# Two fused transformer layers with a product-key stage: the expert choice kept in PSUM, the normalised rows handed to the feature maps in halves across the border of two rounds, four score banks in the last layer-1 pass

## Chip, cores and metric

One core of one Trainium2 chip runs the kernel. The metric is the device time of one execution in microseconds (us), the median of several. TensorE is called PE here, its sequencer PEq and its weight loads PEld, VectorE DVE, ScalarE ACT, GpSimd POOL and SyncE SP, as in the profile.

## What is computed

The input x is 4 batches of 512 rows of 128 numbers. Four blocks follow one another, each with a residual and a layer norm behind it (all float32 in and out):

```python
x = _layernorm(x + _L0_attn_ref(x, ...))   # gated attention in groups of 32 rows, plus a linear part over the batch
x = _layernorm(x + _L0_ffn_ref(x, Wg, We)) # 8 experts, the 2 best per row, weighted
x = _layernorm(x + _L1_attn_ref(x, ...))   # 16 heads of 8, causal linear attention on softmax features
x = _layernorm(x + _L1_ffn_ref(x, ...))    # product keys: top 8 of 32 x 32, rows of down and up
```

In the expert block, `logits = x @ Wg`, the gate is a softmax over 8 experts, the two largest are kept and divided by their sum, and the row's output is the sum of the two chosen experts' products. In the causal attention each head maps q and k by `softmax(p)` and `softmax(-p)` to 16 features, and row t reads the running sum of k (x) v up to t. The last block begins with a batch norm, whose mean and variance run over all 2048 rows.

## The kernel before

The file has two functions with one block of hand-ordered instruction streams each, one stream per engine, which meet by semaphores only. `layers` (lines 184 to 1470) does the first three blocks for all batches, `peer` (from 1474) the last. `layers` takes 320 of the 587 us and is what the change touches.

A batch is T = 4 tiles of 128 rows. Functions `a_*` belong to the gated attention and the experts (layer 0), `b_*` to the causal attention (layer 1). After a prologue that takes batch 0 through layer 0, four rounds follow, `for s in range(1, B + 1)`: round s takes batch a = s through layer 0 and batch b = s - 1 through layer 1, interleaved by hand in each of the four streams. Round 4 has no batch a: it is the lone round. A stream is in order: an instruction that waits holds all that are behind it on its engine.

PSUM has 8 banks. What matters of a round:

- Border. DVE closes batch a with `a_experts(a, p)` (L822, two tiles per p: `z2 = z2 + bank * wexp`, 8 experts), then the norm of z2 (`a_z2`, `a_x2`, L726 to L736, with a `pow` on POOL between, L573), and batch b with `b_y`, `b_z3`, `b_z3_spread`, `b_x3`. PE transposes x2 (`b_x2t`, L1205), ACT copies it, PE multiplies by the combined weights (`b_qkv`, L1217, banks 4 to 7), ACT copies the maps to `pm` (`b_maps`, L414).
- Maps. DVE takes minimum and maximum over each head's 8 numbers (L845, L846), subtracts (L847); POOL subtracts for the negative half (`b_negative`, L600); ACT takes the exponential (`b_exp`, L434); DVE sums, inverts and multiplies to `feat` (`b_features`, L855 to L857). All this for two halves of two tiles.
- In the meantime ACT and PE prepare batch a: `a_qk`, `a_heads` (L359, L369), `a_val`, `a_gate` (L383, L377), `a_sim`, `a_link` (L389), `a_kv` (L1144), `a_outt` (L1153).
- Transposes and low parts. PE transposes features (`b_transposes`, L1231, L1236), ACT copies high halves (L454), DVE computes the low halves `q_lo` (`b_low_queries`, L873).
- Scores. For each tile u and each row group g, PE computes a 128 x 512 score block (`b_scores`, L1267) into bank 4 or 5, DVE masks it (`b_masked`, L883), ACT casts its high half (L463), POOL subtracts for the low half (`b_low_scores`, L622), PE multiplies both with the values (`b_numerators`, L1282 to L1295), DVE sums (`b_summed`, L904). `b_products` and `b_states` (L891, L896) carry the running state from tile to tile.
- Choice. Behind `a_x1`, PE multiplies by Wg (`a_logits`, L1183, bank 1), `a_shift` takes the 8 largest and their places (L786, L792) and marks hits against an iota tile (L797, L799), `a_choice` turns them into weights (L805 to L810). All their small tiles (128 x 32) are in SBUF but the logits. PE computes the experts of tiles 0 and 1 (`a_experts`, L1196) before the second half of `b_scores(b, 2)`.

DVE operations depend on one another through `step`, a semaphore of the engine's own.

## Time and profile before

| | us |
|---|---|
| median of 3 runs | 590.48 (590.31 to 592.97) |
| the profiled execution: its time | 589.03 |
| its span | 587.3 |
| DVE busy | 490.6 (84%) |
| PE busy | 411.7 (70%), mean granted clock 0.764 of 2.4 GHz |
| ACT busy | 317.9 (54%) |
| POOL busy | 189.2 (32%) |

Of the time 1.7 us lie outside the span. A granted clock of 0.50 is 1.2 GHz, 1.00 is 2.4 GHz. In the rows further below, a stretch is given by its start and end from the span's start; a line of a timeline has its start, its duration, engine, line, operation, output<-inputs with their shapes, how many, and in brackets the idle time ahead of it with what ended it. Buffer numbers are left out there, so z and z2, x1 and x2, masked0 (called masked) read alike, and `feat` also holds the masked scores of odd tiles. In the trace the rounds begin at about 66, 134, 200 and 264 us, and `peer` at 320 us.

### The profile page before, as it was taken

The numbers are of one execution on the slowest core, as the hardware profiler recorded it, in microseconds if no ns is written. First come the engines' busy times: TensorE is split into PE (matmuls) and PEld (weight loads), VectorE is DVE, ScalarE is ACT, GpSimd is POOL, SyncE is SP. The second block draws the span as 40 slices with busy tenths as digits, with TensorE's granted clock in tenths as the row PEclk, the third lists the DMA queues.
The fourth block names the chain that finished last, engine by engine and source line by source line (L and its number), as shares of the span: only waits on it lengthen the run. The fifth ranks groups of instructions, "written<-read, shape, count | busy, mean of one in ns | idle before, by whom it ended". The sixth has DMA issues, their size and how long they took to land. (4 is left out here: it accounts for less than half of the span.)

```text
span 587.3 us, 12452 instructions
## 1 busy us (share of the span) xinstructions
PE 411.7 (70%) x4560; PEld 291.7 (50%) x4560; DVE 490.6 (84%) x2056; ACT 317.9 (54%) x639; POOL 189.2 (32%) x211
## 2 busy tenths in 40 slices
PE   1769869986998779854574637576847676767585
PEld 0455548644865467532473214353725354545475
DVE  3586699898999899987854799699979999999991
ACT  0602565346533664314641537767586868688591
POOL 4550224823194416813482230303030303030000
PEclk9998987698859976887755955685959595957577
DMA  7220000000000000000000000000000000000000
GB/s 200 73 61 0 1 2 2 2 1 0 2 0 3 0 2 1 2 1 0 1 2 0 2 1 1 2 2 11 2 10 2 12 2 11 2 11 1 12 2 19
DMA packets 12459, 6.72 MB, mean 11 GB/s; under 512 B 3182, under 2 KB 11758, under 8 KB 12398
## 3 DMA queue, kind: packets, MB, share of 16 engines
q1 hardware_dynamic: 10566, 4.34, 2.8%
q10 hardware_dynamic: 1832, 1.58, 1.0%
q8 instruction: 36, 0.59, 0.4%
q14 instruction: 25, 0.20, 0.1%
HBM read 4.87 MB, written 1.05 MB: 10 GB/s over the span
## 5 line engine op out<-in xcount | busy, mean ns | idle before, releaser
L1665 ACT ACTIVATE hot_last<-iota_f,lo_last 128x128 f16<-128x128 f32 x256 | 75.8, 388 | 0.3 <-DVE lo_last L1789 0.3
L1806 DVE TENSOR_TENSOR hot_lo<-lo_t,iota_lo 128x4096 f16<-128x4096 f16 x24 | 53.6, 2286 | 0.3
L1927 PE MATMUL psum<-hot_w,hot_lo 128*128 128x16 f16 x1536 | 43.6, 172 | 14.0 <-DVE hot_lo L1806 14.0
L1927 PEld LDWEIGHTS psum<-hot_w,hot_lo 128*128 128x128 f16 x1536 | 41.9, 101 | 20.6 <-DVE hot_lo L1806 19.6
L1893 PE MATMUL psum<-x3t,down_t 128*128 128x512 f32 x64 | 42.6, 768 | 13.3 <-ACT hid L1631 11.6
L1579 POOL TENSOR_TENSOR eq<-eq,side_f 128x1024 f16<-128x1024 f16 x14 | 28.9, 2083 | 55.5 <-DVE eq L1767 55.5
L1267 PE MATMUL psum<-q_hi,k_t 32*128 32x128 f16 x256 | 38.0, 259 | 9.8 <-DVE masked L883 6.4
L1587 POOL TENSOR_TENSOR rstd<-rstd,minus_half 128x2 f32<-128x2 f32 x8 | 5.6, 701 | 114.0 <-DVE rstd L1836 114.0
L622 POOL TENSOR_TENSOR s_lo<-masked,s_hi 128x512 f16<-128x512 f32 x32 | 36.5, 1170 | 16.5 <-ACT s_hi L463 12.8
L1736 DVE FIND_INDEX8 side_i<-side,keysims 128x8 uint32<-128x32 f32 x256 | 41.5, 185 | 0.0
L1196 PE MATMUL psum<-we,x1t 128*128 128x512 f32 x64 | 40.1, 777 | 0.4 <-DVE z L822 0.4
L1927 PE MATMUL psum<-hot_w,hot_last 128*128 128x16 f16 x512 | 14.9, 174 | 36.0 <-issue 28.6
L1267 PE MATMUL psum<-q_lo,k_t 32*128 32x128 f16 x256 | 38.2, 261 | 0.0
L1940 PE MATMUL psum<-upw,mix 128*128 128x128 f32 x256 | 36.9, 306 | 1.1 <-DVE mix L1821 1.1
L573 POOL TENSOR_TENSOR a_rstd<-a_rstd,minus_half 128x4 f32<-128x4 f32 x8 | 8.1, 1013 | 90.3 <-DVE a_rstd L731 90.3
L1927 PEld LDWEIGHTS psum<-hot_w,hot_last 128*128 128x128 f16 x512 | 14.4, 104 | 45.1 <-issue 45.1
L622 POOL TENSOR_TENSOR s_lo<-feat,s_hi 128x512 f16<-128x512 f32 x32 | 36.2, 1158 | 1.4 <-ACT s_hi L463 1.4
L1940 PEld LDWEIGHTS psum<-upw,mix 128*128 128x128 f32 x256 | 35.5, 222 | 1.5 <-DVE mix L1821 1.5
L1267 PEld LDWEIGHTS psum<-q_hi,k_t 32*128 32x128 f16 x256 | 25.1, 113 | 17.4 <-DVE masked L883 9.1
L463 ACT CAST s_hi<-masked 128x512 f16<-128x512 f32 x32 | 19.4, 618 | 25.9 <-DVE masked L883 24.9
L1882 PE MATMUL psum<-keysim,xn 128*128 128x512 f32 x32 | 29.1, 1008 | 4.9 <-ACT keysims L1624 4.9
L1893 PEld LDWEIGHTS psum<-x3t,down_t 128*128 128x128 f32 x64 | 13.4, 236 | 35.8 <-ACT hid L1631 23.7
(265 smaller groups left out, 1186.2 us busy)
## 6 DMA issues: line engine op xcount, KB each, us to landing
xall<-in_L_attn_x SPq DMA_DIRECT2D x4, 256.0 KB, 6.9
out<-o SPq DMA_DIRECT2D x8, 128.0 KB, 1.9
we<-in_L_ffn_We SPq DMA_DIRECT2D x1, 512.0 KB, 4.0
downn<-in_L_ffn_down SPq DMA_DIRECT2D x1, 512.0 KB, 5.4
upw<-in_L_ffn_up SPq DMA_DIRECT2D x1, 512.0 KB, 6.5
wh<-in_L_attn_W_h SPq DMA_DIRECT2D x1, 256.0 KB, 4.5
keysn<-in_L_ffn_keys_p ACTq DMA_DIRECT2D x1, 256.0 KB, 10.9
wqkv<-in_L_attn_w_qkv ACTq DMA_DIRECT2D x1, 192.0 KB
```

What stands on the lines that cost most here:

```text
L463: nc.scalar.copy(s_hi[:, u % 2, g, :], masked[u % 2][:, g, :]).then_inc(shi_ok.h, 1)
L622: nc.gpsimd.tensor_tensor(s_lo[:, u % 2, g, :], masked[u % 2][:, g, :], s_hi[:, u % 2, g, :], ALU.subtract).then_inc(slo_ok.h, 1)
L1196: ins = nc.tensor.matmul(bank[Y_BANK[u] + k][:], x1t[:, P * u:P * u + P], v.we[:, 4 * k:4 * k + 4, :].rearrange("p e m -> p (e m)"), start ...
L1267: ins = nc.tensor.matmul(bank[4 + g % 2][:, P * c:P * c + P], k_t[r, u, c, :], q[r, u, c, :], start=(q is q_hi), stop=(q is q_lo))
L1579: nc.gpsimd.tensor_tensor(hit, hit, bc(side_f[:, u % 4].rearrange("p i r h -> p (i r) h").unsqueeze(3), [P, 2 * K, NH, K]), ALU.mult)\
L1665: ins = nc.scalar.activation(hot_last[:, lane], iota_f[:], ACT.Abs, bias=lo_last[:, lane:lane + 1], scale=-1.0)
L1736: ins = nc.vector.max_index(side_i[:, u % 4, s, :], side[:, u % 4, s, :], keysims[:, u % 4, s, :])
L1806: nc.vector.tensor_tensor(hot_lo[:, pairs], bc(lo_t[:, lanes].rearrange("p (j s) -> p j s", s=2).unsqueeze(2), [P, LB // 2, P, 2]), bc(v.i ...
L1882: nc.tensor.matmul(bank[6][:], xn[:, P * (u % T):P * (u % T) + P], v.keysim[:].rearrange("p s k -> p (s k)"), start=True, stop=True)\
L1893: nc.tensor.matmul(bank[H_BANK(b, c)][:], v.down_t[:, c, :], v.x3t[:, N * b:N * b + N], start=True, stop=True).then_inc(h_mm.h, 1)
L1927: ins = nc.tensor.matmul(bank[2 + q][:, c:c + 2 * EH], low, hot_w[:, i, lane // 2, :, :, lane % 2].rearrange("p t e -> p (t e)"), start=(i ...
L1940: nc.tensor.matmul(bank[0][:, P * t:P * t + P], mix[:, EH * t + e, :], v.upw[:, e, :], start=(e == 0), stop=False)
```

## The change

1. **The choice in PSUM.** `logits`, `hits`, `chosen`, `gate_sum` and an iota are slices of bank 6; the iota is put there in each round by a small product in front of the logits. One addition becomes a reduction over the two hits. Logits wait for `b_states` to be through with bank 6, and the experts' second tile no longer waits for the places to be found. `b_states` masks in three pieces, two of them in place in PSUM, and adds from there.
2. **x2 in halves.** `a_z2`, `a_x2`, `b_x2t` and `b_qkv` take a half p (two tiles); x2 has two buffers; the maps' products go to banks 0, 1 (half 0) and 4, 5 (half 1). Half 0 is normalised, transposed and multiplied before the round's end. `b_z3`, its norm and `b_x3`, `b_moments` of batch b - 1 move into the next round, between the halves of the maps. z3 goes to bank 6, the moments read SBUF. ACT takes `a_qk`, `a_heads`, `a_val` and `a_gate` of batch a between the two exponentials, POOL takes `b_negative` before `a_heads`.
3. **The lone round.** Scores use banks 4, 5, 0, 1, and DVE computes the low halves of groups 2 and 3 (`b_low_scores` on DVE), POOL those of 0 and 1 alone.

```diff
+    QKV_BANK = (0, 1, 4, 5)
+    S_BANK = ((4, 5, 4, 5),) * (B - 1) + ((4, 5, 0, 1),)
...
+        logits, iota_t, chosen = (bank[6][:, T * E * k:T * E * k + T * E].rearrange("p (t e) -> p t e", t=T) for k in (0, 1, 4))
+        hits = bank[6][:, 2 * T * E:4 * T * E].rearrange("p (j t e) -> p j t e", j=2, t=T)
+        gate_sum = bank[6][:, 5 * T * E:5 * T * E + T]
...
-                        ins = nc.vector.tensor_tensor(hits[:, j], iota, bc(topi[:, :, j:j + 1], [P, T, E]), ALU.is_equal)
+                        ins = nc.vector.tensor_tensor(hits[:, j], iota_t, bc(topi[:, :, j:j + 1], [P, T, E]), ALU.is_equal)
                     step(ins)
-                    step(nc.vector.tensor_tensor(chosen[:], hits[:, 0], hits[:, 1], ALU.add))
+                    step(nc.vector.tensor_reduce(chosen, hits.rearrange("p j t e -> p t e j"), X, ALU.add))
...
+                def b_low_scores(u):
+
+
+                    for g in (2, 3):
+                        wait(dve, shi_ok, B - 1, 4 * u + g + 1)
+                        nc.vector.tensor_tensor(s_lo[:, u % 2, g, :], masked[u % 2][:, g, :], s_hi[:, u % 2, g, :],
+                                                ALU.subtract).then_inc(slo_last_ok.h, 1)
...
                 def b_states(b):
 
                     wait(dve, st_mm, b)
...
+                    nc.vector.tensor_tensor(state[:, 0], raw[0], own_heads, ALU.mult)
                     for u in range(1, T - 1):
-                        ins = nc.vector.tensor_tensor(state[:, u], state[:, u], state[:, u - 1], ALU.add)
+                        ins = nc.vector.tensor_tensor(raw[u], raw[u], own_heads, ALU.mult)
+                    step(ins)
+                    for u in range(1, T - 1):
+                        ins = nc.vector.tensor_tensor(state[:, u], raw[u], state[:, u - 1], ALU.add)
...
                 def a_logits(b):
 
                     wait(pe, x1t_ok, b)
+                    if b:
+                        wait(pe, st_ok, b - 1)
...
+                    nc.tensor.matmul(iota_t, ones16[:], iota_rows[:], start=True, stop=True)
...
                 def a_experts(b, u):
 
-                    if u == 1:
-                        pe.wait_ge(found_ok.h, b + 1)
-                    elif u == 2 and b:
+                    if u == 2 and b:
...
+                def b_x2t(b, p):
+
+                    if b and p == 0:
+                        wait(pe, sums_ok, b - 1, 3)
+                    for u in (2 * p, 2 * p + 1):
                         wait(pe, x2_ok, b, u + 1)
...
+                def b_transposes(b, u):
+
+                    if u == 0 or u == 2:
+                        wait(pe, twice_ok, b, u // 2 + 1)
+                    if u == 0:
+                        wait(pe, v_ok, b)
```

DVE around the border of rounds 1 and 2, from the sum z3 of batch b to the first maps, before:

```order
L920 TENSOR_TENSOR z<-x,psum 128x512
L726 BN_STATS a_stats<-z 128x6 x4
L729 BN_AGGR a_mv<-a_stats 128x2 x4
L731 TENSOR_SCALAR a_rstd<-a_mv 128x4
L726 BN_STATS b_stats<-z 128x6 x4
L729 BN_AGGR b_mv<-b_stats 128x2 x4
L731 TENSOR_SCALAR b_rstd<-b_mv 128x4
L736 TENSOR_SCALAR x<-z,a_mv,a_rstd 128x128 x4
L736 TENSOR_SCALAR x<-z,b_mv,b_rstd 128x128 x4
L936 BN_STATS bn_raw<-psum 128x6
L845 TENSOR_REDUCE pmin<-pm 128x64
L846 TENSOR_REDUCE pmax<-pm 128x64
```

and with the change, from the y of batch b on:

```order
L946 TENSOR_TENSOR y<-pe_in,den 128x512
L842 SCALAR_TENSOR_TENSOR z<-psum,wexp,x 128x128 x2
L842 SCALAR_TENSOR_TENSOR z<-psum,wexp,z 128x128 x14
L744 BN_STATS a_stats<-z 128x6 x2
L747 BN_AGGR a_mv<-a_stats 128x2 x2
L749 TENSOR_SCALAR a_rstd<-a_mv 128x2
L865 TENSOR_REDUCE pmin<-pm 128x64
L866 TENSOR_REDUCE pmax<-pm 128x64
L867 TENSOR_TENSOR pe_in<-pm,pmax 128x64x8
L754 TENSOR_SCALAR x<-z,a_mv,a_rstd 128x128 x2
L953 TENSOR_TENSOR z<-x,psum 128x512
L875 TENSOR_REDUCE psum_<-pe_in 128x128
```

In front of these rows the change has the statistics of z2's tiles 0 and 1 and their x2; z3's norm, x3 and the moments follow behind the first features.

ACT behind yt (the copy of the transposed y) at the same border, before:

```order
L478 COPY yt<-psum 128x512
L359 ACT_TABLE_LOAD
L359 ACTIVATE qk_t<-psum,bqk_col 128x512
L369 ACTIVATE heads_t<-qk_t,bet,gam 128x512 x2
L383 ACTIVATE val<-psum 128x512
L377 ACTIVATE gate_t<-psum,bh_gate 128x512
L383 ACTIVATE val<-psum 128x512
L409 COPY x2t<-psum 128x512
L483 COPY x3t<-psum 128x512
L414 COPY pm<-psum 128x512 x2
L377 ACTIVATE gate_t<-psum,bh_gate 128x512
L434 ACT_TABLE_LOAD
```

and with the change:

```order
L487 COPY yt<-psum 128x512
L443 ACTIVATE pe_in<-pe_in 128x1024
L416 COPY x2t<-psum 128x256
L365 ACT_TABLE_LOAD
L365 ACTIVATE qk_t<-psum,bqk_col 128x512
L375 ACTIVATE heads_t<-qk_t,bet,gam 128x512 x2
L422 COPY pm<-psum 128x512
L449 ACTIVATE k<-feat 128x32x16
L451 COPY feat<-feat 128x2x16x16
L389 ACTIVATE val<-psum 128x512
L383 ACTIVATE gate_t<-psum,bh_gate 128x512
L389 ACTIVATE val<-psum 128x512
```

The copy of pm, which the first exponential needs, now stands ahead of these rows. Behind them come one more gate, an ACT_TABLE_LOAD and only then the second exponential, the values and the link; before, the second exponential followed the first with four copies between.

DVE in the lone round, from the masks of tile 0 to those of tile 2, with the change:

```order
L905 TENSOR_TENSOR masked<-psum,causal 128x512 x4
L915 TENSOR_TENSOR s_lo<-masked,s_hi 128x512 x2
L905 TENSOR_TENSOR feat<-psum,causal 128x512 x4
L924 TENSOR_TENSOR state<-psum,same_quad 128x144
L926 TENSOR_TENSOR psum<-psum,same_quad 128x144 x2
L929 TENSOR_TENSOR state<-psum,state 128x144 x2
L915 TENSOR_TENSOR s_lo<-feat,s_hi 128x512 x2
L905 TENSOR_TENSOR masked<-psum,causal 128x512 x4
```

Before, the rows `s_lo` are not in this stream: all 16 were on POOL.

## Rows read from the trace of the kernel before

**Rows 1.** Busy time by stretch: us, PE, PEld, DVE, ACT, POOL busy, PEclk, DMA, GB/s.

```profile
226.90:240.40 13.50, 13.42 (x102) 8.95 (x100) 13.07 (x32) 5.41 (x10) 13.22 (x12) 0.57 0.01 1
240.40:251.20 10.80, 9.15 (x162) 6.76 (x160) 9.96 (x26) 3.57 (x6) 6.78 (x6) 1.00 0.01 2
121.93:127.50 5.57, 3.44 (x17) 1.88 (x15) 5.47 (x19) 3.13 (x4) 0.00 (x0) 1.00 0.00 1
121.93:150.79 28.86, 21.38 (x89) 13.63 (x88) 25.96 (x63) 16.70 (x26) 8.54 (x8) 0.88 0.00 1
251.20:284.19 32.99, 14.88 (x82) 9.51 (x80) 27.03 (x68) 13.32 (x23) 6.59 (x6) 0.79 0.00 0
284.19:308.12 23.93, 17.45 (x300) 15.37 (x300) 15.34 (x24) 10.71 (x18) 19.89 (x18) 0.54 0.01 2
322.00:587.00 265.00, 174.83 (x2567) 123.94 (x2565) 233.75 (x1387) 181.27 (x412) 50.68 (x63) 0.70 0.02 6
```

**Rows 2.** VectorE groups 66 to 322 us: count | busy, mean ns | idle before.

```profile
L847 DVE TENSOR_TENSOR pe_in<-pm,pmax 128x512 f32<-128x512 f32 x8 | 8.6, 1076 | 0.3
L896 DVE TENSOR_TENSOR state<-state 128x144 f32<-128x144 f32 x8 | 8.1, 1016 | 0.3
L797 DVE TENSOR_TENSOR hits<-iota_e,topi 128x32 f32<-128x32 f32 x6 | 5.8, 999 | 0.1
...
L845 DVE TENSOR_REDUCE pmin<-pm 128x64 f32<-128x512 f32 x8 | 5.4, 679 | 7.3 <-ACT pm L414 7.3
L799 DVE TENSOR_TENSOR chosen<-hits 128x32 f32<-128x32 f32 x3 | 3.2, 1080 | 0.1
L936 DVE BATCH_NORM_STATS2 bn_raw<-psum 128x6 f32<-128x512 f32 x4 | 2.8, 698 | 4.4 <-ACT x3t L483 4.4
L810 DVE TENSOR_TENSOR wexp<-chosen,lsum 128x32 f32<-128x32 f32 x3 | 2.7, 895 | 0.1
```

**Rows 3.** VectorE timeline, prologue: start, us, instruction.

```profile
49.10 0.29 DVE L797 TENSOR_TENSOR hits<-iota_e,topi 128x32 f32<-128x32 f32 x2
```

**Rows 4.** TensorE timeline, middle of round 3.

```profile
233.75 6.01 PE L1196 MATMUL psum<-we,x1t 128*128 128x512 f32 x8
```

**Rows 5.** VectorE timeline, middle of round 3.

```profile
240.40 1.29 DVE L883 TENSOR_TENSOR masked<-psum,causal 128x512 f32<-128x512 f32 x2
250.09 1.11 DVE L904 TENSOR_REDUCE pe_in<-psum 128x144 f32<-128x432 f32 x2
```

**Rows 6.** GpSimd timeline, middle of round 3.

```profile
244.44 4.50 POOL L622 TENSOR_TENSOR s_lo<-feat,s_hi 128x512 f16<-128x512 f32 x4 [0.35 <-ACT s_hi L463]
```

**Rows 7.** ScalarE timeline, border of rounds 1 and 2.

```profile
126.92 1.52 ACT L369 ACTIVATE heads_t<-qk_t,bet,gam 128x512 f32<-128x512 f32 x2
...
129.99 0.69 ACT L377 ACTIVATE gate_t<-psum,bh_gate 128x512 f32<-128x512 f32 x1 [0.32 <-PE psum L1105]
...
134.15 0.58 ACT L483 COPY x3t<-psum 128x512 f32<-128x512 f32 x1 [1.12 <-PE psum L1316]
...
139.03 1.28 ACT L434 ACT_TABLE_LOAD   x1
140.32 1.06 ACT L434 ACTIVATE pe_in<-pe_in 128x1024 f32<-128x1024 f32 x1
```

**Rows 8.** TensorE timeline, the kv product in rounds 1 and 2.

```profile
76.07 1.99 PE L1144 MATMUL psum<-val,link 128*128 128x256 f32 x8 [2.62 <-ACT link L389]
...
142.18 3.12 PE L1144 MATMUL psum<-val,link 128*128 128x256 f32 x8 [2.62 <-ACT link L389]
146.88 2.08 PE L1153 MATMUL psum<-attn_t,val 128*128 128x128 f32 x8 [1.58 <-DVE attn_t L755]
```

**Rows 9.** VectorE timeline, first low queries in rounds 1 and 2.

```profile
84.69 0.68 DVE L873 SCALAR_TENSOR_TENSOR q_lo<-psum,q_hi 128x512 f16<-128x512 f32 x1
...
150.79 0.68 DVE L873 SCALAR_TENSOR_TENSOR q_lo<-psum,q_hi 128x512 f16<-128x512 f32 x1
```

**Rows 10.** VectorE timeline, last sum of the lone round.

```profile
307.51 0.61 DVE L904 TENSOR_REDUCE pe_in<-psum 128x144 f32<-128x432 f32 x1 [2.95 <-PE psum L1295]
```

More of the change, by code:

```diff
@@ L517, in _ @@
                 a_exp(0)
-                a_qk(1)
-                a_heads(1)
+                b_x2t(0, 0)
                 key_products()
+                b_maps(0, 0)
+                b_values(0, 0)
                 act.wait_ge(pads.h, 2)
@@ L523, in _ @@
                     a, b = s, s - 1
+                    b_exp(b, 0)
+                    b_x2t(b, 1)
+                    if a < B:
+                        a_qk(a)
+                        a_heads(a)
+                    b_maps(b, 1)
+                    b_features(b, 0)
                     if a < B:
@@ L569, in _, with root @@
             def _(pool):
-                def root(var_ok, root_ok, rstd, b, k):
+                def root(var_ok, root_ok, rstd, b, k, tiles=slice(0, T)):
                     wait(pool, var_ok, b, k)
-                    nc.gpsimd.tensor_tensor(rstd[:], rstd[:], bc(v.minus_half[:].unsqueeze(1), [P, T, 1]), ALU.pow)\
+                    nc.gpsimd.tensor_tensor(rstd[:, tiles], rstd[:, tiles],
+                                            bc(v.minus_half[:].unsqueeze(1), [P, tiles.stop - tiles.start, 1]), ALU.pow)\
                         .then_inc(root_ok.h, 1)
@@ L620, in b_low_scores @@
                     for g in groups:
+                        if b == B - 1 and g >= 2:
+                            continue
                         wait(pool, shi_ok, b, 4 * u + g + 1)
@@ L711, in _ @@
                     if a < B:
-                        root(a_var, a_root, a_rstd, a, 2)
-                    root(b_var, b_root, b_rstd, b, 1)
+                        for p in range(2):
+                            root(a_var, a_root, a_rstd, a, 2 + p, slice(2 * p, 2 * p + 2))
+                root(b_var, b_root, b_rstd, B - 1, 1)
             @block.vector
@@ L1133, in a_link @@
                     wait(pe, lin_ok, b, 1)
+                    wait(pe, val_ok, b)
                     for u in range(T):
```

305 lines of the change are left out of this document (169 added, 136 removed).

## Prediction

> **What bounds the kernel now.** I read the page first: DVE is busy 84% of the span, PE 70% at a mean granted clock of 0.764. Then the busy times by stretch, which say what each stretch hangs on. `peer` lasts 265 us (322 to 587, [rows 1]) and is not touched, so all of the difference must arise in the first 320 us. There I cut each round in two. The middle runs from the last x1 to the last of the four sums; in round 3 it is the first two stretches of [rows 1], 13.50 and 10.80 us. The border runs from there to the first `q_lo` of the next round: the fourth stretch, 28.86 us. What follows up to x1 keeps its order, and I cost it at nothing. The lone round is the fifth stretch (border and maps, 32.99 us) and the sixth (scores, 23.93 us).
>
> In the first part of the middle DVE looks full, 13.07 of 13.50 us, but so does PE, 13.42 of 13.50, at a granted clock of 0.57, mostly 1.2 GHz. The PE timeline shows why that matters: the experts take 6.01 us from 233.75 [rows 4], and the scores of tile 2, groups 2 and 3, stand behind them. They come at 240.3, and DVE masks them at 240.40 [rows 5]. The two engines arrive together; a faster DVE would only wait.
>
> In the border DVE is busy 25.96 of 28.86 us. Its waits are those for ACT's `pm`, 7.3 us, and for x3t, 4.4 us, over four borders [rows 2].
>
> **The change, part by part.** *The choice.* A hit costs 999 ns, the addition behind it 1080, the last product 895 [rows 2], while in the prologue two hits take 0.29 us together [rows 3], 0.15 each. Here POOL runs its subtractions all the while (13.22 of 13.50 us busy); there it does not. These rows read two operands from SBUF, while those with a PSUM operand, as the 128x512 mask, keep 0.65 us each beside POOL [rows 5]. The state additions are alike, 1016 ns for 144 columns [rows 2]. With one operand in PSUM I take 0.15 to 0.25 us each: 6 x 0.85 + 3 x 0.9 + 3 x 0.7 = 9.9 us less for the three kinds, and 8 x 0.77 = 6.2 for the states, less 1.6 for the instructions added. That is 14 us of DVE work at least. No row has an output in PSUM; at worst such an instruction stays at 1 us and nothing is saved.
>
> What of it lies on the path is another matter. The experts start behind a chain of PE work at 1.2 GHz: x1 transposes, scores, logits, scores, numerators. All of it stays, in its order; the iota product adds 0.1 us, and the wait of the logits for the states another 0.1. So the masks of 240.40 come when they came, and DVE waits some 4 us ahead of them. From there DVE gets 0.9 us of new work (statistics of two z2 tiles) in front of the last two sums, which it reached at 250.09 [rows 5], 1.2 us after POOL's last subtraction (248.94, [rows 6]): there is no slack for it. Three middles: 3 x 0.9 less small waits = **+2.2 us**. Bounds: +2.9 if nothing is hidden; -6 if PE were no bound, since POOL's own 20.0 us (13.22 + 6.78, [rows 1]) and 2.1 behind it would leave 22.3 of 24.3 us.
>
> *The border.* The halves take both waits out of it: x2's first half is ready before y, and `pm` comes during y and the experts. But ACT's queue has a new order. Call S the end of the last sum and M the end of the first maps. x2 of half 0 with its `pow` 0.8, y and experts 5.57 [rows 1], half a norm 0.9, maps 2.4 (0.68 twice, and 1.08 of L847 [rows 2]): M = S + 9.7. From M ACT must do an exponential (1.06), the copy of half an x2t (0.5), an ACT_TABLE_LOAD (1.28), qk (0.69), two heads (1.52), pm (0.55), two copies of features (1.1), val, gate, val, gate (2.5), a load (1.28), the second exponential (1.0) [rows 7]: 11.4 us. Values and link, 0.8, come next, and only then PE can do kv, the first `a_outt` and the transposes. In round 2 kv took 3.12 and outt 2.08 us, in round 1 kv took 1.99 at 2.4 GHz [rows 8]. With 1.3 for the transposes and 0.6 for `q_hi` that gives M + 19.0 at the lower clock and M + 16.7 at the higher one. I take the lower: PE is idle for some 3.5 us behind `a_sim`, waiting for `a_heads` on POOL, and in round 2 the row with 2.62 us of idle ahead of it is the slow one. S + 28.7 against 28.86 before: **0 us** for the borders of rounds 1 to 2 and 2 to 3; bounds -2.5 each (higher clock) and +2.2 (two copies or a product more in front of the exponential). DVE itself would be ready at M + 15.3, so it waits for `q_lo` in place of `pm`.
>
> *Prologue and round 1.* DVE now waits for the `pow` of half 0 (1.2 us) before the second experts; maps end near 68.0. With 19.0 less 0.5 (no x3t) the first `q_lo` comes at 86.5, at the higher clock at 84.5; before it was 84.69 [rows 9]. I take **+1.5 us**, bounds -0.2 and +3.7.
>
> *Lone round, border.* No layer-0 work stands in ACT's queue, so DVE sets the pace. Before: 32.99 us with 27.03 busy [rows 1], waits 6.0. After: 27.0 less 0.9 (statistics done earlier) plus 0.4 (norms cut in two), and waits of 0.3 (pow), 0.5 (exponential), 0.9 (last two `q_hi`) and 0.4 of issue: 28.6. **-4.4 us**, bounds -5.5 and -3.
>
> *Lone round, scores.* POOL is busy 19.89 of 23.93 us, and the last sum waits 2.95 us for the numerators behind it [rows 1, 10]. POOL loses 8 x 1.13 us (a quarter of 4.50, [rows 6]); DVE gets 8 x 0.6, loses 1.4 in the states, and has 15.34 + 4.8 - 1.4 = 18.7 of work, 1.2 of waits for `s_hi` and 1.7 of numerators at the end: 21.6. But the eight read two SBUF operands beside POOL, and [rows 2] show what that costs: 0.8 us more each at worst for four of them, 24.4. I take the middle, 23.0: **-1.0 us**, bounds -2.3 and +0.5.
>
> The Trainium skill has a rule that speaks against this part (SBUF - State Buffer, "SBUF: two separate sides"): DVE with two SBUF inputs and POOL lock each other out of a shared port for a whole instruction. By that rule the low halves don't run side by side, and the term is +0.5 in place of -1.0. The 999 ns hits fit it; no row has 128x512 subtractions on both engines.
>
> *Sum:* 2.2 + 0 + 1.5 - 4.4 - 1.0 = **-1.7 us**. The profiled execution took 589.03 us and would take 587.3; it lies 1.45 under the median of the runs shown, 590.48, so against that median I forecast **588.8 us**.
>
> **Rivals.** *A, the freed DVE time does arrive.* If PE gets the higher clock through the middle, or through the border, POOL and DVE are the bounds: middles -6 in place of +2.2, borders -5 and -0.2 in place of 0 and +1.5. All of it is -16.6 us, 573.9; half of it, which I hold likelier, about 581. For: PE would have fewer idle stretches at the borders. Against: in three rounds alike the clock was low through the scores and most of the experts (0.57 in [rows 1]). 0.32.
>
> *B, ACT's queue is the new bound, slower than before.* It decides when the second exponential ends later than M + 13: val and gate wait for PE products, which stand behind `b_qkv`, which waits for the x2t copy. Two more microseconds there, in three borders (+2.2, +2.2, and +3.7 in round 1), and the sum is -1.7 + 6.6 = +4.9: 595.4. For: four activations and a table load now stand ahead of it, where four copies stood. 0.17.
>
> *C, the port.* As the term above: +0.5 in the lone round's scores in place of -1.0, 590.3. DVE and POOL alternate. The rule of the skill named there says so. 0.07.
>
> *D, the choice gets no shorter in PSUM.* It lies behind PE as before, so the time stays the forecast's; it is inside the main case.
>
> **How the numbers follow.** Main case 0.44, its own range 585.5 to 592. A difference of 0.5% (2.95 us) is about what a measurement of this kernel tells from none; the bounds are 587.5 and 593.4. Of the main case 0.06 lies under 587.5 and 0.02, its unlikely upper end, over 593.4. Faster 0.06 + 0.32 = 0.38; slower 0.02 + 0.17 = 0.19; same 0.44 - 0.08 + 0.07 = 0.43. The range reaches from half of A to B's value: 580 to 595.5; what is left out is the full A and B's tail.
>
> **What would show it.** Right: hits, additions and states on DVE at 0.15 to 0.3 us; a new wait of 3 to 5 us on DVE ahead of the second masks of tile 2, ended by PE's L1267 counterpart; a wait of 2 us or more ahead of the first `q_lo`, ended by ACT; almost none ahead of pmin; the lone round's border near 28.6 us and its scores near 23. Wrong: x1-to-x1 of rounds 2 and 3 more than 2 us away from 65.8 and 64.7 us; a granted clock of 1.00 through the experts; DVE low halves of 1.5 us or more; `peer` other than 265 us.

## The result, and the profile after

| | before | changed |
|---|---|---|
| median | 591.73 us (4 runs, 590.31 to 593.08) | 582.87 us (4 runs, 580.88 to 586.18) |
| ratio | | 0.9867, 95% interval 0.983 to 0.9904 |
| a second series | 590.33 us (23 runs) | 585.09 us (6 runs, 581.27 to 587.34), ratio 0.9892, 0.9843 to 0.9941 |
| profiled execution: time, span | 589.03, 587.3 us | 583.85, 582.1 us |

The change makes the kernel 1.1 to 1.3% faster: some 5 to 9 us, where 1.7 were forecast. The range, 580 to 595.5, holds it; the central case (own range 585.5 to 592) does not. Ratios are worked out from fast runs alone; one of the fillers kernel's executions further down, at a mean granted clock of 0.55, took 669 us and is not among them.

First the head of the page after. DVE lost 8.5 us of work (490.6 before), although it took over 8.5 us of low halves (4.5 and 4.0, below); PE lost nothing.

```profile
span 582.1 us, 12503 instructions
## 1 busy us (share of the span) xinstructions
PE 411.8 (71%) x4564; PEld 293.6 (50%) x4564; DVE 482.1 (83%) x2076; ACT 314.8 (54%) x643; POOL 182.2 (31%) x208
```

Then the busy times by stretch, cut at the same events as [rows 1]: middle of round 1, border behind it, middle and border of round 2, middle of round 3, the lone round's border and its scores, and the stage `peer`. The columns are those of [rows 1].

```profile
98.30:122.60 24.30, 23.09 (x261) 15.75 (x259) 18.42 (x66) 8.87 (x16) 20.58 (x19) 0.73 0.01 1
122.60:148.90 26.30, 20.20 (x86) 13.72 (x87) 25.27 (x61) 15.95 (x27) 8.21 (x8) 0.87 0.00 0
160.40:184.40 24.00, 23.18 (x260) 16.30 (x260) 18.41 (x66) 8.69 (x16) 20.58 (x19) 0.67 0.01 2
184.40:210.50 26.10, 19.78 (x89) 12.84 (x88) 25.27 (x60) 15.93 (x27) 8.19 (x8) 0.93 0.00 0
222.00:246.10 24.10, 23.28 (x261) 16.33 (x260) 18.52 (x66) 8.69 (x16) 20.59 (x19) 0.67 0.01 2
246.10:274.60 28.50, 16.29 (x89) 10.78 (x89) 26.41 (x63) 13.15 (x24) 6.93 (x6) 0.71 0.00 0
274.60:299.10 24.50, 16.14 (x300) 14.83 (x295) 21.64 (x34) 10.70 (x18) 11.37 (x10) 0.50 0.01 2
311.30:582.10 270.80, 175.86 (x2568) 124.75 (x2568) 234.99 (x1393) 181.95 (x415) 51.85 (x66) 0.69 0.02 6
```

Against before: border 28.9 to 26.3 and 26.1, lone border 33.0 to 28.5, lone scores 23.9 to 24.5, middles 25.4, 24.2, 24.2 to 24.3, 24.0, 24.0 (the windows above are cut to 0.1 us). The last sum of the layers ends at 299.1 us where it ended at 308.1: 9.0 us won. From there to the end it takes 283.0 us where it took 279.2: 3.8 us given back, nearly all in `peer`, of which no instruction was touched.

The groups of DVE answer to [rows 2]: the hits cost 195 ns (999 before), the additions of states 307 (1016), and the wait for `pm` fell from 7.3 to 1.2 us. The low halves, new on DVE, cost 1030 and 1174 ns in the mean (the table says "mean" of single ones that took 0.68 or 1.67 us; see the lone round's scores).

```profile
L865 DVE TENSOR_REDUCE pmin<-pm 128x64 f32<-128x512 f32 x8 | 5.4, 681 | 1.2 <-ACT pm L422 1.2
L815 DVE TENSOR_TENSOR psum<-psum,topi 128x32 f32<-128x32 f32 x8 | 1.2, 195 | 0.1
L929 DVE TENSOR_TENSOR state<-psum,state 128x144 f32<-128x144 f32 x8 | 2.5, 307 | 0.3
L915 DVE TENSOR_TENSOR s_lo<-masked,s_hi 128x512 f16<-128x512 f32 x4 | 4.5, 1174 | 0.2
L915 DVE TENSOR_TENSOR s_lo<-feat,s_hi 128x512 f16<-128x512 f32 x4 | 4.0, 1030 | 1.3 <-ACT s_hi L472 1.2
```

The timelines of round 3's middle answer to [rows 4, 5]: PE's experts, then DVE's last choice instruction, and the second masks of tile 2 behind a wait of 3.30 us. They come 12.1 us behind x1's end, 13.5 before.

```profile
228.81 4.69 PE L1250 MATMUL psum<-we,x1t 128*128 128x512 f32 x8
...
230.65 0.19 DVE L828 TENSOR_TENSOR wexp<-psum,lsum 128x32 f32<-128x32 f32 x1
234.14 1.29 DVE L905 TENSOR_TENSOR masked<-psum,causal 128x512 f32<-128x512 f32 x2 [3.30 <-PE psum L1329]
```

Last, ACT's and DVE's timelines of the border from round 2 to 3: the second exponential, the copies of link and kv, the first `q_hi`, and behind it the first `q_lo`.

```profile
203.82 1.06 ACT L443 ACTIVATE pe_in<-pe_in 128x1024 f32<-128x1024 f32 x1
...
205.04 0.59 ACT L395 COPY link<-psum 128x512 f32<-128x512 f32 x1
...
208.33 0.38 ACT L400 ACTIVATE kv<-psum 128x256 f32<-128x256 f32 x1 [1.64 <-PE psum L1195]
...
209.88 0.60 ACT L463 ACTIVATE q_hi<-psum 128x512 f16<-128x512 f32 x1 [0.57 <-PE psum L1297]
210.51 0.69 DVE L893 SCALAR_TENSOR_TENSOR q_lo<-psum,q_hi 128x512 f16<-128x512 f32 x1 [0.35 <-ACT q_hi L463]
```

### The profile page after: what moved, and what is told of

It reads as the page before. It is cut to its first block and busy times, and to the rows that moved or that the text cites. A ratio compares the mean times of both kernels' runs of the same rounds, so it can differ in the third digit from the quotient of the medians.

```text
span 582.1 us, 12503 instructions
## 1 busy us (share of the span) xinstructions
PE 411.8 (71%) x4564; PEld 293.6 (50%) x4564; DVE 482.1 (83%) x2076; ACT 314.8 (54%) x643; POOL 182.2 (31%) x208
## 5 line engine op out<-in xcount | busy, mean ns | idle before, releaser
L1966 PE MATMUL psum<-x3t,down_t 128*128 128x512 f32 x64 | 43.8, 789 | 13.3 <-ACT hid L1704 11.6
L1652 POOL TENSOR_TENSOR eq<-eq,side_f 128x1024 f16<-128x1024 f16 x14 | 28.9, 2083 | 55.5 <-DVE eq L1840 55.5
L1329 PE MATMUL psum<-q_hi,k_t 32*128 32x128 f16 x256 | 36.5, 260 | 9.1 <-DVE masked L905 7.9
L1329 PE MATMUL psum<-q_lo,k_t 32*128 32x128 f16 x256 | 36.7, 263 | 0.0
L584 POOL TENSOR_TENSOR a_rstd<-a_rstd,minus_half 128x2 f32<-128x2 f32 (+1 forms) x12 | 9.6, 803 | 84.2 <-DVE a_rstd L749 84.2
L636 POOL TENSOR_TENSOR s_lo<-masked,s_hi 128x512 f16<-128x512 f32 x28 | 31.7, 1159 | 11.3 <-ACT s_hi L472 7.6
L636 POOL TENSOR_TENSOR s_lo<-feat,s_hi 128x512 f16<-128x512 f32 x28 | 31.7, 1159 | 6.5 <-ACT s_hi L472 6.5
L1329 PEld LDWEIGHTS psum<-q_hi,k_t 32*128 32x128 f16 x256 | 24.5, 113 | 16.0 <-DVE masked L905 10.4
L1966 PEld LDWEIGHTS psum<-x3t,down_t 128*128 128x128 f32 x64 | 13.9, 244 | 36.4 <-ACT hid L1704 23.9
L1894 DVE SCALAR_TENSOR_TENSOR mix<-psum,hid 128x512 f32<-128x512 f32 x32 | 20.5, 683 | 13.7 <-PE psum L2000 13.7
```

Source lines behind the costliest of these rows:

```text
L636: nc.gpsimd.tensor_tensor(s_lo[:, u % 2, g, :], masked[u % 2][:, g, :], s_hi[:, u % 2, g, :], ALU.subtract).then_inc(slo_ok.h, 1)
L1329: ins = nc.tensor.matmul(bank[S_BANK[b][g]][:, P * c:P * c + P], k_t[r, u, c, :], q[r, u, c, :], start=(q is q_hi), stop=(q is q_lo))
L1652: nc.gpsimd.tensor_tensor(hit, hit, bc(side_f[:, u % 4].rearrange("p i r h -> p (i r) h").unsqueeze(3), [P, 2 * K, NH, K]), ALU.mult)\
L1894: nc.vector.scalar_tensor_tensor(mix[:, :, lanes], bank[2 + q][:].rearrange("p (l e) -> p e l", e=2 * EH), 1.0 / WEIGHT_SCALE, hid[:, b % ...
L1966: nc.tensor.matmul(bank[H_BANK(b, c)][:], v.down_t[:, c, :], v.x3t[:, N * b:N * b + N], start=True, stop=True).then_inc(h_mm.h, 1)
```

## The experiments

Eleven more kernels ran, and the changed one again. Each was cut at the same events; the table gives the us of each stretch in its one profiled execution, worked out from the timelines of DVE: the first `q_lo` of round 1, the three middles (x1's end to the last sum), the two borders (last sum to the next first `q_lo`), the lone round's border (to the first mask of tile 0) and scores (from there to the last sum), the end of the layers' last sum, and from there to the end. The last column is the ratio to the kernel before on the same chip.

| kernel | q_lo | middles | borders | lone | scores | layers' end | rest | ratio (95%) |
|---|---|---|---|---|---|---|---|---|
| before | 84.7 | 25.4 24.2 24.2 | 28.9 28.9 | 33.0 | 23.9 | 308.1 | 279.2 | 1 |
| changed | 86.8 | 24.3 24.0 24.0 | 26.3 26.1 | 28.5 | 24.5 | 299.1 | 283.0 | 0.9867 |
| changed again | 86.7 | 25.0 24.7 24.1 | 25.6 26.5 | 28.3 | 24.5 | 299.9 | 283.4 | 0.9892 (0.9843 to 0.9941) |
| SBUF again | 87.1 | 27.5 26.2 26.2 | 25.6 27.3 | 28.6 | 24.8 | 307.9 | 281.7 | 1.0025 (0.9993 to 1.0058) |
| PSUM alone | 86.9 | 23.8 24.1 24.2 | 28.9 29.0 | 33.0 | 22.9 | 306.9 | 282.6 | 0.9983 (0.9948 to 1.0018) |
| logits in bank 1 | 86.2 | 25.6 25.5 25.2 | 27.3 27.5 | 28.4 | 24.8 | 305.2 | 283.1 | 0.9935 (0.9902 to 0.9968) |
| ACT later | 89.8 | 24.9 24.8 24.7 | 28.6 28.7 | 28.6 | 24.4 | 309.3 | 282.1 | 0.9971 (0.9943 to 0.9999) |
| two banks, POOL | 86.0 | 24.3 24.0 24.7 | 26.2 27.7 | 28.6 | 24.6 | 300.8 | 278.5 | 0.9895 (0.9856 to 0.9934) |
| low halves from PSUM | 87.0 | 24.4 24.0 24.8 | 26.3 27.8 | 28.6 | 23.9 | 301.5 | 278.9 | 0.9869 (0.9843 to 0.9895) |
| lone scores as before | 86.8 | 24.3 24.0 26.4 | 26.2 26.0 | 28.6 | 23.0 | 300.1 | 279.7 | 0.9842 (0.982 to 0.9864) |
| fillers | 87.2 | 24.4 24.4 24.4 | 25.6 25.6 | 28.0 | 24.5 | 298.6 | 282.3 | 0.9845 (0.9804 to 0.9885) |
| link first | 85.9 | 24.7 24.0 25.5 | 27.0 26.8 | 28.6 | 22.9 | 299.2 | 282.9 | 0.9885 (0.9863 to 0.9907) |
| tail shared | 88.3 | 24.6 24.0 24.7 | 26.4 27.8 | 28.6 | 21.3 | 300.3 | 283.7 | 0.9891 (0.987 to 0.9912) |
| link first and tail shared | 84.1 | 24.6 24.0 25.4 | 27.0 26.9 | 28.6 | 20.8 | 295.2 | 279.0 | 0.9874 (0.9832 to 0.9915) |

Rows of code that is the same show how far one execution differs from another: the middle of round 3 is 24.0 to 26.4 us, the border ahead of it 26.0 to 27.8, the first `q_lo` 84.1 to 88.3, the rest 278.5 to 283.7. Differences below 1.5 us in one stretch are read only where several stretches or the lines themselves agree.

### The change once more: what of `peer`?

> The changed kernel once more, on the same chip as the next three. Of the 267.0 us of the peer stage before, 270.8 were measured in the profiled execution with the change, though not one instruction of it was altered. Theory 'phase' (the stage's PE work falls otherwise over the stretches at 1.2 and 2.4 GHz, and that differs from execution to execution): the stage lasts anything from 265 to 271 us here, and its granted clock goes with it, lower where it is longer. Theory 'fixed' (the change costs the stage something of its own): 270 to 271 us again. The layers in front of it should end within 0.5 us of 311.3 in both.

The layers' end was 299.9, 0.8 us behind the first profile (0.5 was expected at most); `peer` was again 4 us long, so this run alone tells nothing apart. The whole table does: from the layers' end on the program is the same in all fourteen profiles but for the place of the last z3 and the source of the last moments (the kernel before and PSUM alone have the old ones), and the rest takes either 278.5 to 279.7 us (before, two banks, low halves from PSUM, lone scores as before, the kernel with both link first and the tail shared) or 281.7 to 283.7 us (the nine others, PSUM alone among them, with none of the halves in it). One place is DVE's wait for PE ahead of a `mix` tile. From the last sum of the layers on it comes at 218.7 us before (526.79 - 308.1) and at 221.6 us after (520.70 - 299.1), of which the wait has 1.7. In order: before, and changed.

```profile
526.79 0.69 DVE L1821 SCALAR_TENSOR_TENSOR mix<-psum,hid 128x512 f32<-128x512 f32 x1 [0.42 <-PE psum L1927]
```

```profile
520.70 0.69 DVE L1894 SCALAR_TENSOR_TENSOR mix<-psum,hid 128x512 f32<-128x512 f32 x1 [2.09 <-PE psum L2000]
```

The other is the end: from the last `mix` on 12.2 us at a granted clock of 0.78 before, 13.0 us at 0.63 after.

```profile
575.10:587.30 12.20, 6.14 (x37) 5.94 (x36) 1.67 (x7) 0.81 (x2) 0.89 (x2) 0.78 0.05 15
```

```profile
569.10:582.10 13.00, 7.04 (x36) 6.85 (x36) 1.62 (x7) 0.81 (x2) 0.89 (x2) 0.63 0.04 12
```

Cut from the layers' end on, the granted clock of the slice from 220 to 240 us is 0.67 in all five short profiles and 0.76 in all nine long ones. So the stretches at 1.2 GHz lie elsewhere in the stage when it is long, which agrees with theory "phase"; and the long kernel with PSUM alone speaks against a cost of the halves. What makes one of the two lengths come is not shown, nor whether the change makes the long one more frequent: of the kernel before there is one profile.

### The choice and the states in SBUF again

```diff
-        hits = bank[6][:, 2 * T * E:4 * T * E]...
+        iota_e, hits, chosen = sb("iota_e", [P, E]), sb("hits", [P, 2, T, E]), sb("chosen", [P, T, E])
-                    nc.vector.tensor_tensor(raw[u], raw[u], own_heads, ALU.mult)
+                    step(nc.vector.tensor_tensor(state[:]..., bank[6][:, 0:(T - 1) * HEADS * VW]..., ALU.mult))
-                        ins = nc.vector.tensor_tensor(state[:, u], raw[u], state[:, u - 1], ALU.add)
+                        ins = nc.vector.tensor_tensor(state[:, u], state[:, u], state[:, u - 1], ALU.add)
```

> The changed kernel with the choice of experts and the state additions in SBUF again; halves, queue orders and lone round as changed. Theory 'halves' (what the change gains it gains in the borders; the time that DVE saves in the choice is a wait for PE): in the three middles 4.7 us of DVE work each come back, 3.3 to 3.7 of them into the wait ahead of the second masks of tile 2, so each middle is 0 to 1.3 us longer, and the whole 0 to 4 us over the change: ratio to the kernel before 0.987 to 0.993. Theory 'choice' (freed DVE time is what arrives): all of it comes back, some 9 us or more, ratio 1.000 or above.

Ratio 1.0025: the whole gain is gone, as theory "choice" said. The middles are 2.2 to 3.2 us longer than in the change; the borders (25.6, 27.3) stay within the scatter of equal code. PE's timeline of round 3 shows the first half of it: the iota product, which stands ahead of the logits in bank 6, waits 1.55 us for the state additions (0.22 in the change). DVE's shows the second: the masks of tile 2 follow the choice without a wait, 14.0 us behind x1's end, though the experts ran in 4.74 us.

```profile
232.08 0.19 PE L1235 MATMUL psum<-iota_rows,ones 128*128 128x32 bf16 x1 [1.55 <-DVE state L925]
...
236.14 4.74 PE L1247 MATMUL psum<-we,x1t 128*128 128x512 f32 x8
...
241.28 0.90 DVE L827 TENSOR_TENSOR wexp<-chosen,lsum 128x32 f32<-128x32 f32 x1
242.22 1.29 DVE L904 TENSOR_TENSOR masked<-psum,causal 128x512 f32<-128x512 f32 x2
```

### The choice and the states in PSUM, and nothing else

The kernel before, with part 1 of the change alone.

> The kernel before with the choice of experts and the state additions in PSUM, and nothing else of the change. Theory 'halves': DVE is 14 us less busy and the time the same within 0.3%, since the masks of tile 2 wait for PE; x1 to x1 in rounds 2 and 3 within 1 us of 65.8 and 64.7. Theory 'choice': 583 to 586 us, ratio 0.985 to 0.99, x1 to x1 some 3 us shorter. Hits 0.15 us each beside POOL in either.

Ratio 0.9983, x1 to x1 64.1 and 64.6 us (65.8 and 64.7 before; the 1.7 us of the first lie in the middle of round 1 and were not expected): theory "halves" for the time. Up to the first `q_lo` this kernel is 2.2 us longer. Part of that is a wait that the move to bank 6 brought: in the prologue the logits now come 1.0 us later behind x1, since the bank must first be read out by the copy of `keys_t`. DVE waits 4.67 us, as the prediction had it for this part, while the experts run for 6.05.

```profile
47.23 0.19 PE L1198 MATMUL psum<-iota_rows,ones 128*128 128x32 bf16 x1 [1.76 <-DVE keys_t L1005]
...
233.46 6.05 PE L1210 MATMUL psum<-we,x1t 128*128 128x512 f32 x8
...
240.16 1.29 DVE L889 TENSOR_TENSOR masked<-psum,causal 128x512 f32<-128x512 f32 x2 [4.67 <-PE psum L1281]
```

So neither part is worth anything alone (1.0025 with the halves and the lone round's part, 0.9983 with PSUM), and together they give 1.1 to 1.3%. The next run shows why.

### SBUF, and the logits in their old bank

```diff
-        logits, iota_t = (bank[6][:, ...]... for k in (0, 1))
+        logits = bank[1][:, 0:T * E].rearrange("p (t e) -> p t e", t=T)
-                        wait(pe, st_ok, b - 1)
+                    if u == 1:
+                        pe.wait_ge(found_ok.h, b + 1)
```

> As the kernel with the choice in SBUF again (ratio 1.0025 to the kernel before), but the logits go to their old bank, so they no longer wait for the state additions, and the numerators of tile 1 don't wait for the choice. Theory 'bank' (what the PSUM choice gives is that the logits' new bank is free soon enough: there PE waited 1.55 us ahead of the iota product for the additions in SBUF): the middles of rounds 2 and 3 fall from 26.3 to 25.0 us or less, ratio 0.993 to 0.998. Theory 'DVE' (the masks of tile 2 wait for the SBUF choice itself): middles 26 us or more, ratio as before.

The middles fell to 25.6, 25.5 and 25.2 us, the ratio to 0.9935 (the intervals of the two kernels don't touch). Theory "bank" holds for 0.7 to 1.9 us of each middle (the edit took away two waits together, that of the logits for the states and that of tile 1's numerators for the choice). What is left over the change and its repeat, 0.6 to 1.5 us each, is the SBUF choice itself: in round 3 PE's experts ended at 238.99, DVE's last choice instruction at 240.15 us, and the masks of tile 2 follow it without a wait.

### ACT later

```diff
+                    for k in range(3):
+                        nc.scalar.copy(spare[:, k], x1t[:]).then_inc(spare_ok.h, 1)
                     b_exp(b, 1)
```

> The changed kernel with three more copies of 128x512 (some 1.7 us) on ACT ahead of the second exponential of each round; their output is used by nobody. In the changed kernel that exponential ends 1.2 us ahead of DVE's sum behind it. Theory 'DVE bounds the border': 1.2 us are hidden and each of the three borders with layer-0 work gets 0.5 to 0.9 us longer, the whole 1.5 to 3 us, as the vparts, link and kv behind it come later too. Theory 'ACT's queue bounds it' (rival B of the prediction): the full 1.7 us in each border, the whole 5 us or more.

Round 1 got 3.0 us longer up to its first `q_lo`, the borders 2.4 and 2.6, for 1.67 us of copies; the ratio moved from 0.987 to 0.997. Theory "ACT's queue" holds, and by more than its full 1.7. The timelines of ACT, PE and DVE show the way it takes: not by the exponential, for which DVE waits 0.26 us, but by the copy of link, for which PE sits idle 2.27 us; and the kv products behind it then take 3.23 us in place of 2.61. (That last part is the clock's: in the repeat, with kv at 3.0 us, this border was 26.5 us, and against it 2.2 us remain.)

```profile
209.26 1.67 ACT L549 CAST spare<-x1t 128x512 f16<-128x512 f32 x3
...
213.34 1.22 DVE L879 TENSOR_REDUCE psum_<-pe_in 128x128 f32<-128x1024 f32 x1 [0.26 <-ACT pe_in L444]
...
213.46 0.59 ACT L396 COPY link<-psum 128x512 f32<-128x512 f32 x1
...
214.10 3.23 PE L1199 MATMUL psum<-val,link 128*128 128x256 f32 x8 [2.27 <-ACT link L396]
...
219.98 0.69 DVE L897 SCALAR_TENSOR_TENSOR q_lo<-psum,q_hi 128x512 f16<-128x512 f32 x1 [2.37 <-ACT q_hi L464]
```

### Link ahead of the exponential

```diff
+                    if a < B:
+                        a_link(a)
                     b_exp(b, 1)
                     b_values(b, 1)
-                    if a < B:
-                        a_link(a)
```

This kernel and the two further down that share the tail start from the one with the lone scores as before.

> The kernel with the lone round's scores as before (ratio 0.984), and on ACT the copy of link goes ahead of the second exponential instead of behind it. Theory 'ACT's way to kv bounds the border' (three added copies ahead of link made each border 2.5 us longer): link is copied 0.6 us earlier and the first q_lo comes 0.3 to 0.6 us earlier in each of the three borders, the whole 1 to 2 us. Theory 'DVE bounds it': the exponential comes 0.6 to 1.2 us later, DVE waits for it, and the time is the same or up to 2 us worse.

Counted from the first exponential (193.79 us here, 193.94 in the change) link was copied 0.7 us earlier, but DVE now waits 1.10 us for the exponential, and the borders are 27.0 and 26.8 us against 26.2 and 26.0. Theory "DVE bounds it". The kernel that shares the tail as well has 27.0 and 26.9. With the run before it: in the changed border ACT's and DVE's chains are both at the bound, and moving this one instruction ahead gains nothing.

```profile
204.16 0.58 ACT L395 COPY link<-psum 128x512 f32<-128x512 f32 x1 [1.79 <-PE psum L1172]
206.05 1.06 ACT L443 ACTIVATE pe_in<-pe_in 128x1024 f32<-128x1024 f32 x1
...
207.14 1.22 DVE L873 TENSOR_REDUCE psum_<-pe_in 128x128 f32<-128x1024 f32 x1 [1.10 <-ACT pe_in L443]
```

### The lone round's scores: four kernels

Two banks, all low halves on POOL, the order of the change:

```diff
-    S_BANK = ((4, 5, 4, 5),) * (B - 1) + ((4, 5, 0, 1),)
+    S_BANK = ((4, 5, 4, 5),) * B
-                        if b == B - 1 and g >= 2:
-                            continue
-                        b_low_scores(0)
```

> The changed kernel with the lone round's scores as before: two score banks, all sixteen low halves on POOL. Theory 'port' (DVE's eight subtractions of two SBUF operands cost 1.1 us each beside POOL, which eats what POOL is relieved of): the lone round's scores take 23.4 to 24.4 us against 24.4, so the time is that of the change within 1 us, or up to 1 us better. My forecast's theory (sharing the low halves is worth 1 us): it is 1 us worse. Border of the lone round 28.6 us in both.

24.6 us: the four banks and DVE's eight subtractions gain nothing, in line with theory "port". But the kernel with PSUM alone had done it in 22.9 us. Its orders were still those of before: the states between the two halves of tile 1's masks. So that was tried. The edit also puts PE's scores and numerators of this stretch back into the order of before (not shown here):

```diff
-                        b_masked(b, 1)
+                        b_masked(b, 1, (0, 1))
                         b_states(b)
+                        b_masked(b, 1, (2, 3))
```

> The changed kernel with the lone round's scores quite as in the kernel before: two banks, low halves on POOL, state additions (in PSUM) between the two halves of tile 1's masks, and PE's order of scores and numerators as before. In the kernel with PSUM alone this stretch took 22.9 us, with POOL at work from its first subtraction to its last; in the changed kernel 24.5. Theory 'the lone part costs': 22.5 to 23.3 us here, the time 1 to 2 us under that of the change. Theory 'it pays or is even': 24 us or more.

23.0 us, ratio 0.9842, the lowest here, though its interval overlaps with the change's. Two orders changed together; POOL's timelines point to DVE's. With the change's order (first fence) POOL waits 1.49 us for the rounding of the states, which DVE computes only behind all of tile 1's masks; with the order of before (second) it has no gap, and its 19.85 us are the stretch but for 3.2.

```profile
282.22 2.26 POOL L634 TENSOR_TENSOR s_lo<-feat,s_hi 128x512 f16<-128x512 f32 x2
285.97 1.00 POOL L640 TENSOR_TENSOR state<-state,state_parts 128x432 f32<-128x432 f32 x1 [1.49 <-ACT state_parts L477]
```

```profile
283.05 2.28 POOL L634 TENSOR_TENSOR s_lo<-feat,s_hi 128x512 f16<-128x512 f32 x2
285.28 1.00 POOL L640 TENSOR_TENSOR state<-state,state_parts 128x432 f32<-128x432 f32 x1
```

Third, the change with the masked scores of groups 2 and 3 left in PSUM for DVE's low halves:

```diff
-  masked[u % 2][:, g, :]
+  bank[S_BANK[B - 1][g]][:]
```

> The changed kernel, but in the lone round the masked scores of groups 2 and 3 stay in their PSUM banks: DVE multiplies by the mask in place, ACT rounds from PSUM, and DVE's low halves read one operand from PSUM and one from SBUF. Theory 'two SBUF operands beside POOL' (a DVE instruction with two SBUF operands and a POOL instruction run one after the other): the eight low halves take 0.65 to 0.75 us each in place of 1.13, and the lone round's scores 21 to 23 us in place of 24.5. Theory 'longer by themselves': 1.1 us each here too, 24.5 us or more. Either way PE's second and later scores of these groups wait for a subtraction, which can give back 0.5 us.

The same subtraction on the same engine, in the change (first) and here (second): a pair takes 2.27 us with two SBUF operands, 1.29 with one in PSUM, and POOL keeps 1.13 for one of its own in both. 23.9 us for the stretch: a gain of 0.6, since DVE then waits for ACT's rounding (1.15 to 1.60 us, three times).

The pairs of the change taken apart settle whether two SBUF operands are slow by themselves. POOL's second subtraction ran from 277.19 to 278.34. DVE's first began at 277.21 and ended at 278.88, 0.54 us behind POOL's; its second, with POOL idle, took 0.68. So DVE stands still until POOL is through, and alone it has the speed of the kernel with PSUM. In the third pair and the fourth it is the same (1.67 and 0.68). In the second DVE's first takes 1.10 us behind the last 0.55 us of a POOL addition, its second 0.68, and POOL's next addition 1.29 where it takes 1.00 in the kernel with PSUM: there POOL waits for DVE.

```profile
277.19 1.15 POOL L636 TENSOR_TENSOR s_lo<-masked,s_hi 128x512 f16<-128x512 f32 x1
277.21 1.67 DVE L915 TENSOR_TENSOR s_lo<-masked,s_hi 128x512 f16<-128x512 f32 x1
278.81 0.68 DVE L915 TENSOR_TENSOR s_lo<-masked,s_hi 128x512 f16<-128x512 f32 x1
```

```profile
280.15 1.29 DVE L917 TENSOR_TENSOR s_lo<-psum,s_hi 128x512 f16<-128x512 f32 x2
...
291.40 1.29 DVE L917 TENSOR_TENSOR s_lo<-psum,s_hi 128x512 f16<-128x512 f32 x2 [1.40 <-ACT s_hi L473]
```

Fourth, both lessons together: lone scores as before, but DVE takes two of the last tile's low halves from PSUM, alone and with link first.

> The kernel with the lone round's scores as before (23.0 us for that stretch, POOL at work without a gap), but of its last tile DVE does two of the four low halves, reading the masked scores in PSUM. If POOL's subtractions are the bound of this stretch, it ends 2.0 to 2.3 us earlier, 20.7 to 21.2 us, and the whole is 2 us shorter (ratio 0.980 to 0.982). If PE's last numerators at 1.2 GHz or ACT's rounding bound it, less than 1 us comes of it.

> Both of the last two edits together. The two lie in different stretches, so their gains should add: the ratio is the one with the lone round as before, 0.984, less 0.004 for the tail and 0 to 0.003 for the link.

The stretch took 21.3 and 20.8 us against 23.0, as expected, POOL busy 17.63 of 21.30. The ratios don't show it: 0.9891 and 0.9874 against 0.9842, where 0.980 to 0.982 and less were expected. In the profile of the first, the prologue was 1.5 us longer (first `q_lo` 88.3) and the rest 4.0 us longer (283.7) than in the kernel it starts from, more than the 1.7 won. The second was profiled in an execution of 575.98 us (84.1, and 279.0 for the rest), the lowest of its six, of which another was 577.05 and four were over 584. The gain in the stretch is shown; that it reaches the median is not.

### Fillers on PE

```diff
+                        fill(8)
                         a_sim(a)
+                        fill(4)
                         a_link(a)
+                        if u == 0 and g == 2:
+                            wait(pe, ft_ok, b)
+                            fill(2)
```

> The changed kernel with products that nobody reads (bf16, 128x512, into bank 7) where PE sat idle: eight ahead of a_sim, four ahead of a_link, two between the halves of the first tile's scores. Theory 'idle time lowers the clock' (the low stretch in the border and the one that starts 1 to 2 us ahead of x1's end follow PE's idle stretches): the granted clock is 1.00 through link and kv, and the low stretch in the middle is shorter or gone, then the middles fall from 24 toward 22 us and the whole by up to 5 us. Theory 'busy time lowers it' (the low stretch of the middle comes behind a stretch of full PE work at 1.00): the low stretches stay as long or get longer, more PE work at 1.2 GHz, and the whole is 0 to 4 us longer. Where a filler is still running when a_sim could start, that costs up to 1 us per border in either.

Half and half. In the border from round 2 to 3 the granted clock is 1.00 from end to end (0.93 in the change), kv takes 1.99 us in place of 2.61, and both borders are 25.6 us: 0.4 and 0.6 shorter than in the change, and just what the repeat had from round 1 to 2, where its kv took 1.99 too. The low stretch of the middle stayed (0.63 from 222 to 235, 0.66 in the change), and the middles are no shorter. The ratio, 0.9845, can't be told from the change's.

```profile
184.60:210.30 25.70, 20.53 (x100) 12.85 (x101) 25.20 (x61) 16.17 (x27) 8.45 (x8) 1.00 0.00 1
222.00:235.00 13.00, 11.97 (x100) 7.97 (x98) 7.94 (x35) 5.33 (x11) 12.82 (x12) 0.63 0.01 2
```

## Where the prediction was right and where it was wrong

Term by term, all from the profiled execution:

| term | predicted | measured | |
|---|---|---|---|
| three middles | +2.2 | -1.6 | wait right, clock wrong |
| borders 1 to 2, 2 to 3 | 0 | -5.4 | the wrong one of two clocks, and 1 us too much at that one |
| prologue and round 1 | +1.5 | +1.9 | size right, cause in part another |
| lone border | -4.4 | -4.5 | right |
| lone scores | -1.0 | +0.6 | wrong end of the bounds |
| `peer` and what is around it | 0 | +3.8 | taken as fixed |
| sum | -1.7 | -5.2 | |

*The borders.* "M = S + 9.7" was measured as 9.5 (184.4 to 193.9 in round 3's border), and the first `q_lo` came at M + 16.6, where the text had "M + 16.7 at the higher" and chose "M + 19.0 at the lower". The step that failed is "I take the lower". Its reason was PE's idle time behind `a_sim` for `a_heads`; measured were 2.58 us ahead of `a_sim`, for ACT's val, and 1.22 behind it (0.30 in the border from round 1 to 2). Link and part of kv did run at 1.2 GHz, but kv took 2.61 us, not 3.12, and everything behind it ran at 2.4 GHz. That 16.6 met 16.7 is in part luck: link was copied 0.5 us earlier than reckoned, and kv took 0.6 longer than the 1.99 of the higher clock. The fillers, at 1.00 throughout, give only 0.4 to 0.6 us more, so most of the distance between the two clocks had been won already.

The other branch came too, in code that is the same: with two banks, with low halves from PSUM and with the tail shared, kv of the border from round 2 to 3 ran wholly at 1.2 GHz (3.78 us). There the first `q_lo` waits 2.0 us for ACT, as the prediction had it, but comes at M + 18.3, and these borders are 27.7 and 27.8 us, 1.1 under the kernel before. So the forecast of 0 was too high even at its own clock (the terms that it gives for the lower clock add up to 19.3, not 19.0), and 1.7 of the 5.4 us hang on the clock of one execution. The two lines are those of two banks.

```profile
204.82 3.78 PE L1179 MATMUL psum<-val,link 128*128 128x256 f32 x8 [0.52 <-ACT link L395]
211.33 0.69 DVE L891 SCALAR_TENSOR_TENSOR q_lo<-psum,q_hi 128x512 f16<-128x512 f32 x1 [2.03 <-ACT q_hi L463]
```

*Prologue and round 1.* The first maps ended at 69.3 us, not "near 68.0", and the first `q_lo` came 17.5 us behind them, not 18.5; the two errors nearly cancel. Of the first, 1.0 us is a wait of the logits in the prologue for the copy of `keys_t` out of bank 6, which the sum had at nothing, and which the kernel with PSUM alone has too. With 84.1 to 88.3 us for equal code, this term's agreement says little.

*The middles.* The wait of "some 4 us" stands ahead of the masks of tile 2 (3.3 to 3.7 us, 3.5 to 4.4 in the repeat). "So the masks of 240.40 come when they came" failed: the low stretch that begins a little ahead of x1's end ended at 231 us, 9 us behind x1, where it had lasted to 238.3, 11 us behind it. The experts took 4.69 to 5.11 us in place of 5.92 to 6.39, and the 0.9 us of new statistics was more than paid. In the repeat they took 4.90 to 5.83 and the middles 24.1 to 25.0. Round 3's middle, the same code in six further kernels, shows what hangs on it: experts of 5.6 us go with a middle of 24.7 or 24.8, experts of 6.2 to 6.4 us with 25.4 to 26.4, up to 2.2 over the kernel before. So with the experts at the low clock a middle is 1.2 to 2.2 us longer than before, more than the 0.9 forecast; in the profile of the change that case did not come.

*"D, the choice gets no shorter in PSUM: it lies behind PE as before, so the time stays the forecast's"* is the step that failed most. It was argued from the PE chain of before. In the changed kernel the logits share bank 6 with the states; with the additions in SBUF PE stands still 1.55 us ahead of them, DVE arrives last at the masks of tile 2, and the 0.9 us of statistics come on top. The SBUF kernel lost the whole gain, 6.1 to 7.7 us of it in the middles. Logits in bank 1 gave 3.6 of these back: so much was the bank. The other 2.5 to 4.1 us are DVE's own time in the choice and the states, which the forecast took to lie behind PE.

*The lone scores.* Term C was to be "+0.5 in place of -1.0": +0.6 was measured, a pair of DVE's halves at 2.27 us. The rule of the Trainium skill (SBUF - State Buffer, "SBUF: two separate sides") is borne out by DVE's subtractions of two SBUF operands, 1.67 us where POOL's ran and 0.68 where POOL was idle, and by the kernel with the operand in PSUM, 0.65 us. The prediction set the middle between rule and no rule; it had the 999 ns hits as evidence and should have taken the rule. It also overlooked the price of the order: 1.5 us on POOL when the states move behind all masks of tile 1. So the agreement with C's figure is in part luck: with all halves on POOL the order of before gives 23.0 us and that of the change 24.6, and only against the latter does the sharing gain nothing (24.5). (The prediction's upper case, 21.6 and four times 0.8, is 24.8, not 24.4.)

*Rivals.* A, "the freed DVE time does arrive", gave 573.9 in full and 581 for half; 582.9 lies next to the half. Its borders came in full in this profile (-5.4 against "-5"), its middles hardly (-1.6 against "-6"). B did not happen, but its mechanism is real: 1.67 us more in ACT's queue cost 2.4 to 3.0 us in each round with layer-0 work. Its point was set on the wrong instruction: with the copies the second exponential ended at M + 12.5, before "M + 13", and the border had already lost 2.6 us, because link and kv stand behind it. The chance of faster was 0.38 where 0.43 stood for the same; the two clocks of the border, each a plain reading of [rows 8], decided most of it.

*Signs.* Two of those named for wrong came: x1 to x1 of rounds 2 and 3 was 62.1 and 61.6 us (65.8 and 64.7), and `peer` was longer. Of those for right, hits and additions (0.20, 0.31 us), the wait ahead of the second masks and the lone border (28.5) came; the wait ahead of the first `q_lo` was 0.5 and 0.4 us in rounds 2 and 3, not 2.

## What to carry to other kernels

Two edits can be worth nothing each and 1% together: when one moves data to a place that is released later, and the other makes the release early, price the pair, and undo one of them in the changed kernel, not only add it to the old. When a term hangs on which of two clocks a stretch gets, give both branches their own chance in place of a central value. On a queue, look for the last instruction that someone on another engine waits for: it was link, two copies behind the exponential that was watched.
